# A feature-interaction network on one core: the first pair's broadcast operands made by TensorE instead of by DMA

## The reference, cut to what matters

```python
x0 = xk = emb                                        # (b, 26, 32)
for w, bb in ((conv1_w, conv1_b), (conv2_w, conv2_b)):
    hp = jnp.einsum('bhd,bmd->bhmd', xk, x0).reshape(-1, h * M, E)
    xn = jax.nn.sigmoid(jnp.einsum('oi,bid->bod', w, hp) + bb[None, :, None])
    xk = xn[:, :half]; res.append(xn[:, half:])
cin_out = (concat(res, 1).sum(-1) @ cin_w + cin_b)[:, 0]
h1 = tanh(deep_x @ W1 + b1); h2 = tanh(h1 @ W2 + b2); h3 = tanh(h2 @ W3 + b3)
y = linear_out + cin_out + (h3 @ deep_w + deep_b)[:, 0] + bias[0]
```

## Time and profile before

| | us |
|---|---|
| median of 3 runs | 420.84 (420.27 to 423.86) |
| the profiled execution | 420.59 |
| its span in the trace | 418.8 |
| TensorE busy in the span | 402.7 |
| granted TensorE clock, mean of the span | 0.992 |

### The profile page before, as it was taken

One profiled execution on the slowest core, in us unless ns is written; L12 is line 12 of the kernel. 1 busy time (PEld: TensorE's weight loads), 2 busy tenths in 40 slices (PEclk: granted clock), 3 DMA queues, 4 the chain that ended last, 5 costly groups with the idle time before them and its releaser, 6 DMA issues.

```text
span 418.8 us, 5255 instructions
## 1 busy us (share of the span) xinstructions
PE 402.7 (96%) x1854; PEld 167.9 (40%) x1854; DVE 311.9 (74%) x347; ACT 161.9 (39%) x269; POOL 174.6 (42%) x146
## 2 busy tenths in 40 slices
PE   3967999999999999999999999999999999999998
PEld 1412233333333333333333333333333335887885
DVE  4104869998989989898989898998989898432223
ACT  3136445435253544544543525354454511112012
POOL 6745473664844754855656600000000255880000
PEclk9979999999999999999999999999999999999999
DMA  5368689999999999999989998899978670430000
GB/s 203 60 142 177 159 185 227 212 237 235 216 230 224 220 236 237 224 235 212 234 227 219 228 226 233 211 221 214 227 189 200 167 186 2 122 79 2 1 0 2
DMA packets 43582, 73.93 MB, mean 177 GB/s; under 512 B 22206, under 2 KB 24638, under 8 KB 43555
## 3 DMA queue, kind: packets, MB, share of 16 engines
q1 hardware_dynamic: 39970, 71.82, 71.5%
q0 software_dynamic: 3584, 1.76, 3.2%
HBM read 71.63 MB, written 1.71 MB: 175 GB/s over the span
## 4 chain that ended last, share of the span: by engine, by line
PE 88%; issue 4%; ACT 2%; another core or an unknown queue 2%; DMA 1%; SPq 1%; DVE 1%; DVEq 0%; ACTq 0%
PE conv L495 43%; PE conv L473 19%; PE conv L516 8%; PE ring L516 7%; PE ring L485 5%; PE ring L455 4%; ACT xk L660 1%; SPq L319 1%; PE ring L531 1%; ACT x L632 1%; DMA idx_sb<-in_idx 0%; ACT res L662 0%; DMA copied<-emb 0%; DVE prod L836 0%
## 5 line engine op out<-in xcount | busy, mean ns | idle before, releaser
L396 POOL DMA_INDIRECT emb<-in_table,rows x112 | 141.9, 1267 | 96.9 <-DMA emb<-in_table,rows 65.2
L836 DVE TENSOR_TENSOR prod<-ring,xk 128x1024 f32<-128x1024 f32 x96 | 114.2, 1216 | 32.3 <-ACT xk L660 27.4
L836 DVE TENSOR_TENSOR copied<-copied,xk 128x1024 f32<-128x1024 f32 x112 | 135.1, 1243 | 0.0
L495 PE MATMUL conv<-copied,w_sb 128*64 128x512 f32 x448 | 105.2, 593 | 0.0
L660 ACT ACTIVATE xk<-conv,const_sb 64x512 f32<-64x512 f32 x64 | 43.7, 683 | 143.1 <-PE conv L473 117.0
L495 PE MATMUL conv<-prod,w_sb 128*64 128x512 f32 x384 | 93.1, 605 | 2.7 <-DVE prod L836 2.7
L473 PE MATMUL conv<-sq,w_sb 117*64 117x512 f32 x384 | 90.7, 608 | 3.4 <-ACT sq L689 3.4
L495 PEld LDWEIGHTS conv<-copied,w_sb 128*64 128x64 f32 x448 | 31.7, 137 | 63.5 <-issue 55.8
L473 PEld LDWEIGHTS conv<-sq,w_sb 117*64 117x64 f32 x384 | 27.7, 139 | 58.8 <-issue 57.7
L405 POOL TENSOR_TENSOR xt_lo<-xt,xt_hi 128x512 fp32r<-128x512 f32 (+1 forms) x7 | 10.9, 1582 | 96.2 <-ACT xt_hi L726 91.6
L649 ACT ACTIVATE sq<-ring 117x512 f32<-117x512 f32 x90 | 48.6, 595 | 3.9 <-issue 3.2
(11 more groups left out here) (99 smaller groups left out, 324.8 us busy)
## 6 DMA issues: line engine op xcount, KB each, us to landing
copied<-laid SPq DMA_DIRECT2D x224, 256.0 KB
wpiece<-in_mlp SPq DMA_DIRECT2D x22, 256.0 KB
raw<-laid SPq DMA_DIRECT2D x56, 52.0 KB
emb<-in_table,rows POOLq DMA_INDIRECT x112, 4.8
laid<-emb SPq DMA_DIRECT2D x16, 96.0 KB
sel_f<-in_sel SPq DMA_DIRECT2D x1, 832.0 KB, 5.6
const_sb<-in_const SPq DMA_DIRECT2D x1, 626.5 KB, 4.1
w_sb<-in_w SPq DMA_DIRECT2D x1, 416.0 KB
```

The costliest lines, as they stand in the source:

```text
L396: pool.indirect_dma_start(out=emb[0:n, i, j, :], out_offset=None, in_=table, in_offset=bass.IndirectOffsetOnAxis(ap=rows[0:n, i, j:j + 1], ...
L495: mm = nc.tensor.matmul(conv[i % 2][c * HALF:(c + 1) * HALF, :], w2_sb[:, t, :], prod_of(r)[:, c, :], start=(t == 0), stop=(t == T2 - 1))
L836: nc.vector.tensor_tensor(prod_of(r)[:, :, :].rearrange("p c n -> p (c n)"), left[:, :, :].rearrange("p c n -> p (c n)"), xk[i % 2][:, :, ...
```

## The change

All thirteen left operands of pair 0 are now spread by TensorE. Its rows are no longer laid out in DRAM, and the broadcasting copies begin with pair 1: the first six fill the six `copied` buffers. So that all thirteen fit, the order of pair 0 on TensorE is written anew: three spreads stand before `layer1(0, 1)`, and each later one stands before the main matmul of the tile three before it. `WARM` goes from 12 to 9, and of the two matmuls at line 562 one is left.

```diff
-WARM = 12
+WARM = 9
+        def is_copied(r):
+            return r >= T2 and r % T2 in COPIED
         def spreads_up_to(r):
-            return NS * (r // T2) + SPREAD.index(r % T2) + 1
+            return r + 1 if r < T2 else T2 + NS * (r // T2 - 1) + SPREAD.index(r % T2) + 1
...
         for u in range(UT):
             enter(("sums", 0, u))
-        enter(("spread", SPREAD[0]))
-        enter(("spread", SPREAD[1]))
+        for r in range(UT):
+            enter(("spread", r))
         for u in range(UT):
             enter(("sums", 1, u))
-        for r in SPREAD[2:]:
+            enter(("spread", UT + 2 * u))
+            enter(("spread", UT + 2 * u + 1))
+        for r in range(3 * UT, T2):
             enter(("spread", r))
...
             direct(0)
-            lay_out(0)
-            for n in range(2):
-                copy(n)
             direct(1)
             lay_out(1)
-            for n in range(2, RC):
-                copy(n)
             lay_out(2)
             fetch(2)
+            for n in range(RC):
+                copy(n)
...
             for i in range(NPAIR):
                 if i < KW:
                     load_piece(i)
+                if i == 0:
+                    lay_out(RX)
+                    fetch(RX)
+                    continue
...
             layer1(0, 0)
             pe.wait_ge(sel_done, 2)
-            spread_tile(SPREAD[0])
-            spread_tile(SPREAD[1])
+            for t in range(UT):
+                spread_tile(t)
             layer1(0, 1)
             pe.wait_ge(w2_in, 16)
             slot_free("sums", 1, 0)
-            for k in range(2):
+            for k in range(1):
                 nc.tensor.matmul(sums_bank(1, 0)[:, 0, :], ...)
             for u in range(UT):
                 sums_of(1, u)
-                main(u)
-            spread_tile(SPREAD[2])
-            main(3)
-            spread_tile(SPREAD[3])
+                for t in range(2 * u, 2 * u + 2):
+                    spread_tile(UT + t)
+                    main(t)
             layer1(1, 0)
-            for r in SPREAD[4:-1]:
-                spread_tile(r)
-            for t in range(4, 8):
+            for t in range(2 * UT, T2 - UT):
+                spread_tile(UT + t)
                 main(t)
-            spread_tile(SPREAD[-1])
             layer1(1, 1)
-            for t in range(8, T2 - 1):
+            for t in range(T2 - UT, T2 - 1):
                 main(t)
```

More of the change, by code:

```diff
@@ L220, in build, with laid_landed @@
         wide = [copied[RC - DIRECT + k] for k in range(DIRECT)]
+        def laid_landed(i):
+            return LAID * (i // RX + (1 if i % RX else 0))
         def raw_landed(i):
@@ L238, in squares_up_to @@
             return UT * c + u + 1 if i == 0 else 2 * (UT * i + u) + c + 1
+        def is_copied(r):
+            return r >= T2 and r % T2 in COPIED
         def spreads_up_to(r):
-            return NS * (r // T2) + SPREAD.index(r % T2) + 1
+            return r + 1 if r < T2 else T2 + NS * (r // T2 - 1) + SPREAD.index(r % T2) + 1
         def copies_up_to(r):
-            return NC * (r // T2) + COPIED.index(r % T2) + 1
+            return NC * (r // T2 - 1) + COPIED.index(r % T2) + 1
         def tile_of_copy(n):
-            return T2 * (n // NC) + COPIED[n % NC]
+            return T2 * (n // NC + 1) + COPIED[n % NC]
         def tile_of_spread(n):
-            return T2 * (n // NS) + SPREAD[n % NS]
+            return n if n < T2 else T2 * ((n - T2) // NS + 1) + SPREAD[(n - T2) % NS]
         def prod_of(r):
-            if r % T2 in COPIED:
+            if is_copied(r):
                 return copied[(copies_up_to(r) - 1) % RC]
@@ L322, in fetch @@
             def fetch(i):
-                sp.wait_ge(laid_in[i % RX], LAID * (i // RX + 1))
+                sp.wait_ge(laid_in[i % RX], laid_landed(i))
                 if i < RX:
@@ L366, in _ @@
                     load_piece(i)
+                if i == 0:
+                    lay_out(RX)
+                    fetch(RX)
+                    continue
                 for k in range(NC):
-                    n = NC * i + RC + k
+                    n = NC * (i - 1) + RC + k
                     if k == FETCH_AT and i + RX < NPAIR:
                         fetch(i + RX)
-                    if n < NC * NPAIR:
+                    if n < NC * (NPAIR - 1):
                         copy(n)
@@ L638, in x_high @@
                 else:
-                    act.wait_ge(spread_done, NS * (i - RX + 1))
+                    act.wait_ge(spread_done, T2 + NS * (i - RX))
                 nc.scalar.activation(x[i % RX][0:XEND, :], raw[i % RX][0:XEND, :], ACT.Copy)\
@@ L822, in _ @@
                     r = i * T2 + t
-                    n = copies_up_to(r) - 1 if t in COPIED else spreads_up_to(r) - 1
+                    n = copies_up_to(r) - 1 if is_copied(r) else spreads_up_to(r) - 1
                     if t == 0:
@@ L827, in _ @@
                         dve.wait_ge(xk_ready, 4 * (i + 1))
-                    if t in COPIED:
+                    if is_copied(r):
                         dve.wait_ge(copy_in[n % RC], 32 * (n // RC + 1))
```

## The result

| | us |
|---|---|
| the kernel before, median of 4 runs beside the changed one | 421.55 (420.27 to 423.86) |
| the changed kernel, median of 4 runs | 437.25 (436.41 to 438.25) |
| ratio | 1.036, 95% interval 1.0318 to 1.0403 |
| the profiled execution, its span | 436.41, 434.6 |

A forecast was written before the change was run, and what follows sets the result against it. The prediction took TensorE, busy throughout the loop, as the bound. A start 10.28 us earlier and a pair 0 4.04 longer made -6.24, so the median of 420.84 became 414.6 us, range 413.3 to 419.0.

The forecast's parts named there:

- the late signals: TensorE's signals to pair 0's squares and second sigmoid, blamed on copies the change removes; gains 3.09 and 2.57 us.
- a third term: Layer 1 of pair 0 at full instead of half clock, given no idle stretch of TensorE; gain 2.60 us.
- Sums at 19.2: Sums of pair 0 start at 19.2 instead of 21.53 us with three fewer warm matmuls; gain 2.33 us.
- Squares 0.54 behind: Pair 0's squares start 0.54 us after its sums instead of 3.63; gain 3.09 us.
- layer 1 in 2.8 us: The first twelve layer 1 records of pair 0 take 2.8 us instead of 5.4; gain 2.60 us.
- sigmoid at 27.1: Pair 0's second sigmoid starts at 27.1 us, directly after `x_high(1)`; gain 2.57 us.
- product at 28.5: Pair 0's first product starts near 28.5 us, the start having gained 10.28 us in sum.
- The term for the direct DMAs: At the start, `x_high(1)` waits for pair 1's direct DMAs until 25.80 instead of 25.49 us; loss 0.31 us.
- Pair 0 longer by 4.04: From first product to marker, seven more spreads, an unhidden matmul and small waits cost 4.04 us, bounds 3.0 and 5.0.
- the first rival: TensorE's clock falls in the 3.15 us gap before the first product, losing 3.4 us: 418.0 us, chance 0.28.
- Copies and rows of pairs 1 to 3 hidden, 0: Pair 1's copies arrive by 52 us, pair 3's rows at about 57.8; priced at 0, with a bound of 2.
- late signals in pair 0, or late signals that have nothing to do with copies: TensorE's late signals delay pair 0's spreads (422.4 us) or the start's gains fall out (422.8 us); chance 0.10.

The follow-up runs named there:

- e3: Changed kernel with pair 2's gathers waiting for the first product and pair 1's copies issued before its rows: 433.26 us, ratio 1.0274.
- e7: Changed kernel with the gather of pair 3 waiting for the seventh product: 436.81 us, ratio 1.0335.
- e5: Changed kernel with rows of pairs 2 and 3 loaded by SP with ordinary DMAs instead of GpSimd's gathers (other values): 425.27 us, ratio 0.9976.
- e9: Changed kernel with rows of pairs 1 to 4 loaded by SP with ordinary DMAs instead of gathers (other values): 415.69 us, ratio 0.9805.
- e10: Kernel before with rows of pairs 1 to 4 loaded by SP with ordinary DMAs instead of gathers: 418.5 us, ratio 0.9884.
- e12: Kernel before, but from pair 3 on a gather waits for the rows two pairs back instead of one: 532.57 us, ratio 1.2595.
- e13: Changed kernel with GpSimd writing one 1x512 tile and waiting for it after each gather instruction of pairs 2 and 3: 423.94 us, ratio 1.0024.
- e15: Kernel before with GpSimd writing one 1x512 tile and waiting for it after each gather of pairs 2 and 3: 419.35 us, ratio 0.9934.
- e17: Changed kernel with GpSimd writing one 1x512 tile and waiting after each gather instruction of pairs 1, 2 and 3: 420.65 us, ratio 0.9952.
- e2: Changed kernel with the direct DMAs of pair 1 issued only after all squares of pair 0: 442.94 us, ratio 1.0504.
- e1: Changed kernel with 12 warm matmuls and two fillers, as in the kernel before: 452.05 us, ratio 1.0719.
- e4: Changed kernel with the layout of pair 0's rows and four operand copies put back, into memory nobody reads: 429.61 us, ratio 1.0187.
- e8: Kernel before with nine warm matmuls instead of twelve and one filler instead of two ahead of pair 1's sums: 422.83 us, ratio 0.9977.
- e18: Kernel before with GpSimd writing one 1x512 tile and waiting after each gather of pairs 1, 2 and 3: 422.11 us, ratio 1.0008.
- e16: Kernel before with GpSimd writing two 1x512 tiles and waiting after each gather of pairs 2 and 3: 426.26 us, ratio 1.0106.

## Why the prediction was wrong

**The step that failed** is the cause of the late signals, which the prediction used twice ("by the copies that the change takes away", 3.09 and 2.57 us) and on which a third term hung (2.60, the clock). I read them beside a DMA share of 0.98 in the earlier trace rows and took the neighbour for the cause. The cause is GpSimd's gathers; that row shows GpSimd busy for only 0.37 of 2.00 us, which hid them, for the signals came at 25.14, 2.8 us after pair 1's last gather had ended. That the gathers hold the signals is shown from five sides: the signals are prompt between gathers (e3, and e7 at a DMA share of 1.03), prompt where ordinary DMAs bring as many rows (e5, e9, e10), held for 65 us where gathers follow without a break (e12), released by 0.5 us pauses (e13, e15, e17), and, but for e2's first and e1's last, as late or later with more work for TensorE or with other DMAs moved (e1, e2). The Trainium skill, DMA: Bandwidth & Descriptors, section "SWDGE vs HWDGE vs iDMA", says that for a DMA from GpSimd its own cores write each descriptor into rings in SBUF, and that DMAs issued from SP or ScalarE never take that path. The runs agree as far as they go: SP's loads of as many rows hold nothing. By what road those writes would reach TensorE's signals no page states and no run here shows.

**Why the change made it worse**, when the gathers were there before. Shown: the copies and `lay_out(0)` put back (e4) return the first product to 38.14. In the traces, copies delay the landing of pair 1's gathers, and with it the start of pair 2's: 27.07 in the kernel before, 26.5 in e4, 24.71 in the changed kernel; and under load the gathers that run hold less (`layer1(0, 0)` is prompt in both kernels with the load, 6.51 late without). It isn't only how long the gathers have run: in e2, without the load, `layer1(0, 0)` ends 3.4 us into pair 2's gathers and is signalled 8.23 late, while in e12, with it, a spread that ends 5.3 us into them is signalled in 0.02. That the load itself does this, and how, is only argued; in e1 sums that end 1.6 us later move the holds by 2 to 4 us.

**Step by step.**

- Sums at 19.2: 19.44 measured. Right, but worth nothing alone (e8).
- Squares 0.54 behind, layer 1 in 2.8 us, sigmoid at 27.1, product at 28.5: 3.98 behind, 6.4 us in three pieces at 1.2 GHz, 46.09, 47.51. With no gathers in the way all four are right (0.53, 2.79, 27.13 and 28.55 in e9). Sizes and order were sound; their condition was not met. That e9 meets 28.53 to 0.02 is in part luck: its second sigmoid waits for line 500, which ends at 27.08 (26.75 in the forecast), and not for `x_high(1)`, since SP had brought pair 1's rows early. The term for the direct DMAs, 0.31, stands untested: the two runs in which `x_high(1)` waits for them, e17 (0.89) and e18 (1.07), have slower gathers.
- Pair 0 longer by 4.04: without holds 25.98 - 20.43 = 5.55 (e9). Of that, 1.7 is the first rival, 3.4 us at clock 0.50 behind a gap of 2.84; the rest, 3.85, is the term. In e17 the low stretch was 6.8 us, with TensorE busy for 4.47 of them, and pair 0 6.1 longer. In the changed kernel it was 7.13 longer; from 48.88 to 53.70 TensorE was busy throughout at clock 0.51, which makes 2.4 of it by my estimate, and the last 0.9 stays unexplained.
- Copies and rows of pairs 1 to 3 hidden, 0: right. From the first product of pair 1 to that of pair 2 the changed kernel takes 18.78 us, as before (18.79); there the copies had 22 us more than the forecast gave them, but e17, with its marker at 56.9, takes 18.77.
- So even where nothing is held the changed kernel is not faster at the marker: it gains 2.76 at the start and loses 5.55 in pair 0 (e9 against e10). It still ends 2.8 us earlier, because the kernel before waits for copies behind the marker, which the forecast didn't reckon with: less than half of the 6.24, and by another road. With pauses alike it is e17 against e18, 0.9952 against 1.0008, and against the best of the kernel before, e15, 0.9952 against 0.9934, both with intervals that overlap: no gain of the change over the best kernel before can be told.
- The rival "late signals in pair 0, or late signals that have nothing to do with copies" was the right one and had 0.10. It priced their return at the old size, 422.8, and put the most that one late signal costs at 2.6, though the sum above it had one of 3.09; they grew, those of layer 1 alone from 2.25 to 6.51 and 10.69.

Open: what in a gather holds a signal, whether the pause itself or the lower rate of gathers lets it out (no run separates them; in e12 two single steps of 2.2 us, at 121.8 and 124.0, did not free the signal that was held from 88.1), and what the load changes in it.

## What to carry to other kernels

When a profile shows "remote" or an unnamed releaser although the producing matmul is long over, compare the semaphore's own time with the end of the matmul, and look at what GpSimd issues in that stretch before you blame the DMA load. Where GpSimd gathers while others wait for single signals of TensorE, try a pause of half a us behind each gather, and watch that the rows still come in time (with longer or more pauses e16 and e18 lost in pair 1 what they had gained at the start), or let the gathers wait for each other as here; the one wait that looked idle, for the rows of the pair before, is worth 110 us. And a change that puts more of a critical path on one kind of signal should be priced with the worst that the trace shows of that signal, not with its best.

## What was not expected of the hardware

- TensorE's signals can be held for as long as GpSimd issues gathers back to back: 64.7 us (e12). They come out 0.7 to 3.5 us behind the last gather (e12, e3), or one by one.
- Memory writes of 0.51 us between gathers (one gather every 1.74 us instead of 1.25) take layer 1's holds of 6.51 and 10.69 us down to 0.74 and 0.02.
- Copies of 256 KB at the same time hold nothing by themselves (e7, share 1.03), and need not add to the holds: with them and pair 2's gathers, `layer1(0, 0)` is signalled in 0.01 us (e4).
- A gap of 2.84 us without a matmul was followed by 3.4 us at 1.2 GHz (e9), where 2.73 before had no such sequel.
